# A graph layer with mixing attention and experts: scales of a group three stages late and fuller long rounds under the sort, contiguous one-hots, another end of layer two

## The reference

```python
xn = layernorm(x)
# graph part, two layers: mean over incoming edges, a linear layer, layer norm, SiLU
agg = segment_sum(h[src], dst) / maximum(degree, 1)
h = silu((layernorm(agg_plus_h @ W.T + b)) * g + beta)        # agg_plus_h = h + agg
# mix part (8 heads of 64): k, v = xn @ w_kv ; k and v are normalized over the 64 of each head
dots = sum_n k[n, h, :, None] * v[n, h, None, :]; out = (q @ dots / N) @ w_out.T + b_out
x = x + h + out
# experts: xf = layernorm(x); ONE routing decision from the mean of all rows of xf
logits = mean(xf) @ Wr + br                # softmax twice, the best 2 of 8 experts
x = x + layernorm(weighted sum of two experts' gelu MLPs(xf) + xf) * gamma + beta
```

## Time and profile before

| | us |
|---|---|
| median of 3 runs | 3044.67 (3039.23 to 3049.11) |
| the profiled execution | 3043.2 |
| its span in the trace | 3041.4 |
| DVE / PE / ACT / POOL busy | 1900.6 / 2552.5 / 1417.6 / 171.0 |

### The profile page before, as it was taken

How to read it: one execution, slowest core, us unless ns; L and a number is a source line. 1 busy time by engine, 2 the same in 40 slices (tenths; PEclk the granted TensorE clock), 3 DMA queues, 4 the chain that set the end, 5 groups by cost and what they waited for, 6 DMA issues and landing times. The chain is left out here.

```text
span 3041.4 us, 50876 instructions
## 1 busy us (share of the span) xinstructions
PE 2552.5 (84%) x14238; PEld 1577.4 (52%) x14238; DVE 1900.6 (62%) x4816; ACT 1417.6 (47%) x3756; POOL 171.0 (6%) x161
## 2 busy tenths in 40 slices
PE   1775664858688888889999999997999999968997
PEld 0343343424344454446578888884444444445665
DVE  8888978899899999999643222221333333355555
ACT  1875565257566666678622222222222222235665
POOL 0000000000000000000000000000111111114000
PEclk9888887889899999999999999998999999978999
DMA  5000000012144344344364444445444444401000
GB/s 179 18 18 9 15 15 15 35 61 98 73 156 149 114 154 144 120 148 141 139 226 144 154 147 145 149 143 194 136 136 140 135 136 138 140 1 38 28 21 30
DMA packets 167927, 318.02 MB, mean 105 GB/s; under 512 B 30227, under 2 KB 139540, under 8 KB 167764
## 3 DMA queue, kind: packets, MB, share of 16 engines
q1 hardware_dynamic: 115860, 230.55, 23.5%
q10 hardware_dynamic: 51776, 85.24, 7.7%
q0 software_dynamic: 128, 0.26, 0.0%
HBM read 203.09 MB, written 112.92 MB: 104 GB/s over the span
## 5 line engine op out<-in xcount | busy, mean ns | idle before, releaser
L1194 PE MATMUL banks<-outer,ring 128*128 128x512 f16 x2450 | 544.8, 381 | 16.0 <-DMA outer<-table,heavy 9.0
L825 ACT ACTIVATE ring<-banks 128x512 f16<-128x512 f32 (+1 forms) x637 | 367.0, 576 | 340.5 <-POOLq L676 337.3
L1191 PE MATMUL banks<-tabs,ring 128*128 128x257 f16 x2250 | 497.3, 273 | 2.5 <-DMA ring<-counts 2.5
L1192 PE MATMUL banks<-tabs,ring 128*128 128x256 f16 x2250 | 497.2, 272 | 0.0
L1194 PEld LDWEIGHTS banks<-outer,ring 128*128 128x128 f16 x2450 | 239.4, 98 | 302.3 <-issue 23.2
L826 ACT ACTIVATE banks<-banks 128x512 f32<-128x512 f32 (+1 forms) x637 | 368.6, 579 | 0.0
L1849 DVE TENSOR_SCALAR ring<-val,outer 128x512 f16<-128x512 f16 x1102 | 316.0, 345 | 39.6 <-PE banks L1157 38.7
L1157 PE MATMUL banks<-ring 128*128 128x512 f16 x920 | 270.4, 409 | 66.7 <-SPq L565 31.7
L969 PE MATMUL banks<-tabs,xT 128*128 128x512 f32 x400 | 201.9, 652 | 54.2 <-ACT xT L734 54.2
L1191 PEld LDWEIGHTS banks<-tabs,ring 128*128 128x128 f16 x2250 | 218.7, 97 | 32.7 <-DVE big L1887 2.2
L1192 PEld LDWEIGHTS banks<-tabs,ring 128*128 128x128 f16 x2250 | 219.5, 98 | 26.8
(11 more groups left out here) (368 smaller groups left out, 3939.4 us busy)
## 6 DMA issues: line engine op xcount, KB each, us to landing
counts<-ring ACTq DMA_DIRECT2D x84, 896.0 KB, 4.1
ring<-counts SPq DMA_DIRECT2D x94, 800.0 KB, 4.7
ring<-counts SPq DMA_DIRECT2D x94, 768.0 KB, 4.0
outer<-in_fw SPq DMA_DIRECT2D x8, 1024.0 KB, 8.1
outer<-in_x SPq DMA_DIRECT2D x5, 1280.0 KB, 13.5
x_transposed<-xT SPq DMA_DIRECT2D x50, 128.0 KB, 1.7
outer<-in_x SPq DMA_DIRECT2D x25, 256.0 KB, 2.9
xT<-x_transposed SPq DMA_DIRECT2D x25, 256.0 KB, 2.7
```

Of the source, the lines that this page charges most:

```text
L825: act.activation(held[:, b, 0:q, c, :], cell_bank.rearrange("p (q r) -> p q r", r=P), ACT.Copy, scale=0.25).then_inc(s_cell, 1)
L1191: mm(o[:, 0:D + 1], a, xtab[l][:, cb, D:2 * D + 1], start=cb == 0, stop=False)
L1192: m = mm(o[:, 0:D], a, xtab[l][:, cb, 0:D], start=False, stop=cb == NT - 1)
L1194: m = mm(o, a, xtab[l][:, cb, 0:2 * D], start=cb == 0, stop=cb == NT - 1)
```

## The change

Three parts, independent of each other.

**Mix under the sort.** `kv_norms` is cut in two: `kv_sums` (1503 and 1505 of before) stays at its tick; `kv_scales` (reciprocal and the multiplications of k) stands three ticks later in DVE's queue (in the rounds, right behind the sums as before). ACT's square root of a row window is moved behind the squares of the next window's first tile. The tiles of the rounds are dealt out anew: 4 to each of the odd rounds 1 to 11, and 2 to rounds 10, 12 and 13. PE has the dots of a window no longer ahead of the next even round's second turn half, but between the products of the tiles of the next odd round.

**One-hots.** `hot_c` is laid out with the column innermost, so that a step's weights are contiguous; `iota_c` is now 0..127 once, `col_v` holds every value twice (so that the innermost run of both inputs has two elements, the second input one value twice, and the value is read again for each of the 64 pairs).

**End of layer two.** The transposes of pair 23 stand inside the columns of the last tiles and its product behind those of tile 48; DVE's order for the last two pairs is written out; the affine of the last pair's normed rows is finished on DVE and not on POOL; xf's transposes use three banks in place of four; nine pairs (0 to 8) are transposed before the mean, 16 (9 to 24) behind the router's logits on PE, behind the third exponential on ACT and behind the routing weights on DVE.

```diff
+SCALE_LAG = 3
-WINDOWS = [2] * ROW_WINDOWS + [0, 3, 0, 3, 1, 3, 1, 3, 2, 3, 3, 3, 3, 2]
+WINDOWS = [2] * ROW_WINDOWS + [0, 4, 0, 4, 0, 4, 0, 4, 0, 4, 2, 4, 2, 2]
...
+XF_BANKS = (0, 1, 3)
+XF_LOWS = ((0, 2), (2, 3), (3, 5), (5, 7), (7, 9))
+XF_EARLY = XF_LOWS[-1][1]
...
                     kv_squares(t)
+                    if t == WSTART[w] and 0 < w < ROW_WINDOWS:
+                        kv_stds(w - 1)
...
             for w in range(ROW_WINDOWS):
                 window(w)
-                kv_stds(w)
+            kv_stds(ROW_WINDOWS - 1)
...
-                if w >= ROW_WINDOWS:
-                    dots_to(WSTART[w])
+                if WINDOWS[w] == 0:
+                    return
                 for t in range(WSTART[w], WSTART[w + 1]):
                     dots_to(t - 4)
                     kv_product(t)
...
+                if tick - SCALE_LAG in NORM_AT:
+                    kv_scales(NORM_AT[tick - SCALE_LAG])
                 if tick in NORM_AT:
-                    kv_norms(NORM_AT[tick])
+                    kv_sums(NORM_AT[tick])
...
-        hot_c = [v.bitcast(F16).rearrange("p (c k) -> p c k", k=8) for v in (ringf[:, 0:512], ringf[:, 512:1024], fvec[:, 0:512])]
+        hot_c = [v.bitcast(F16).rearrange("p (k c) -> p k c", k=8) for v in (ringf[:, 0:512], ringf[:, 512:1024], fvec[:, 0:512])]
...
-                dve.tensor_scalar(col_v[:, q % 2, 0:n], bank[5][:, 0:n], -64.0 * PB[q], None, op0=ALU.add)
+                dve.tensor_scalar(col_v[q % 2][:, 0:n, :], bank[5][:, 0:n].unsqueeze(2).to_broadcast([P, n, 2]), -64.0 * PB[q], None,
+                                  op0=ALU.add)
...
-                    dve.tensor_tensor(hot_c[t // 8 % 3], iota_c,
-                                      col_v[:, q % 2, u:u + 8].unsqueeze(1).to_broadcast([P, P, 8]), op=ALU.is_equal)
+                    dve.tensor_tensor(hot_c[t // 8 % 3].rearrange("p k (c u) -> p k c u", u=2),
+                                      iota_c.unsqueeze(1).to_broadcast([P, 8, P // 2, 2]),
+                                      col_v[q % 2][:, u:u + 8, :].unsqueeze(2).to_broadcast([P, 8, P // 2, 2]), op=ALU.is_equal)
...
-            dense(1, NP - 1, 0, 0, 0)
+            agg_free(1, NP - 1, 0)
+            slab_in(1, NP - 1, 0, 0)
+            columns(1, NP - 1, 0, 0, range(0, 12))
+            z_transposes(1, NP - 2, 1)
+            columns(1, NP - 1, 0, 0, range(12, HALF)).then_inc(s_half[1], 1)
+            product(1, NP - 2, 1)
             dense(1, NP - 1, 0, 0, 1)
...
-            for p in range(16, NP):
-                xf_transposes(p)
...
             mm(bank[6][:, 0:NE], ones[0:1, :], br_s[:, :], start=False, stop=True).then_inc(s_lg, 1)
+            for p in range(XF_EARLY, NP):
+                xf_transposes(p)
...
+            def last_pairs():
+                p, q = NP - 2, NP - 1
+                z_low(1, p, 1)
+                normal_h(1, p, 1)
+                z_tile(1, q, 0, 0)
+                dve.tensor_copy(stage[0][:, D:2 * D], tile(xn, NT - 1)).then_inc(s_z[1], 1)
+                outcome_sums(p, 1)
+                z_low(1, q, 0)
+                outcome_scaled(p, 1)
...
+                dve.tensor_tensor(two(tile(xn, q * 2, 2)), two(tile(xn, q * 2, 2)), both(gvec[1][1]), op=ALU.add).then_inc(s_gb[1], 1)
...
             link(dve.tensor_tensor(tw[1], e8[:, 0:1], tw[0], op=ALU.mult))
+            for p in range(XF_EARLY, NP):
+                xfT_low(p)
```

More of the change, by code:

```diff
@@ L709, in _ @@
             residual_beta(0)
-            with pool.Fori(2, NP) as p:
+            with pool.Fori(2, NP - 1) as p:
                 affine(1, p)
@@ L806, in _ @@
             act.wait_ge(s_nrm, NT)
-            act.activation(iota_c, iota16[:, 0:P].unsqueeze(2).to_broadcast([P, P, 8]), ACT.Copy, scale=0.5).then_inc(s_conv, 1)
+            act.activation(iota_c.rearrange("p c u -> p (c u)"), iota16[:, 0:P], ACT.Copy, scale=0.5).then_inc(s_conv, 1)
             for n, (a, scale) in enumerate(((0, 1.0), (2, 64.0), (1, 0.5))):
@@ L862, in xfT @@
                 act.wait_ge(s_ft, p + 1)
-                act.activation(xfp[:, p * 2:p * 2 + 2, 0:D], two(bank[p % 4]), ACT.Copy, scale=X_SCALE).then_inc(s_fc, 1)
+                act.activation(xfp[:, p * 2:p * 2 + 2, 0:D], two(bank[XF_BANKS[p % 3]]), ACT.Copy, scale=X_SCALE).then_inc(s_fc, 1)
             for n in range(2):
@@ L881, in second_layer @@
             def second_layer(p, b):
-                last = isinstance(p, int) and p == NP - 1
+                if isinstance(p, int) and p == NP - 1:
+                    zT(1, p, b)
+                    deviations(2, p - 1, 1 - b)
+                    for n in range(*XF_LOWS[0]):
+                        xfT(n)
+                    h_rows(1, p, b)
+                    deviations(1, p, b)
+                    for n in range(*XF_LOWS[1]):
+                        xfT(n)
+                    for n in range(*XF_LOWS[2]):
+                        xfT(n)
+                    silu(1, p)
+                    for n in range(*XF_LOWS[3]):
+                        xfT(n)
+                    deviations(2, p, b)
+                    return
                 zT(1, p, b)
-                if last:
-                    for n in range(4):
-                        xfT(n)
                 h_rows(1, p, b)
@@ L889, in second_layer @@
                 silu(1, p)
-                deviations(2, p, b)
+                if not isinstance(p, int) or p < NP - 2:
+                    deviations(2, p, b)
             pairs(act, second_layer)
-            for p in range(4, NP):
+            act.activation(small[:, 316:317], small[:, 317:318], ACT.Exp)
+            for p in range(*XF_LOWS[4]):
                 xfT(p)
-            act.activation(small[:, 316:317], small[:, 317:318], ACT.Exp)
             for n in range(3):
```

85 lines of the change are left out of this document (56 added, 29 removed).

## The result

| | before | changed |
|---|---|---|
| median | 3044.3 us (3039.23 to 3049.11, 4 runs) | 3011.68 us (3009.86 to 3013.41, 4 runs) |
| profiled execution, its span | 3043.2, 3041.4 us | 3013.41, 3011.7 us |

The ratio is 0.9893, 95% interval 0.9875 to 0.9911: the change makes the kernel 1.1% faster. I compare the two traces by five marks that both have.

A forecast was written before the change was run, and what follows sets the result against it. DVE's work bounds row stage, rounds and steps, a chain of small operations the end of layer two; 9 + 13 - 1 + 16 = 37 off 3043.2 gives 3006.2, as median 3008 us, range 2992 to 3025.

The forecast's parts named there:

- Row stage, 9 forecast: Row windows of the sort: moving scales and root lets 9 us of DVE's 12.9 us wait go, bounds 4 to 13.6.
- The wait for the squares: Row stage: DVE's wait in the sums for ACT's last squares falls from 12.9 to about 3 us.
- Rounds, 13 forecast (10 to 23): Rounds of the sort: redealt tiles and moved dots gain 13 us; 23 if the dots cost nothing, 10 if more.
- The pitch of 6.3: Odd rounds: dots between products add about 1 us to each tile's pitch, 6.3 in place of 5.15 us.
- the wait in the sums: Rounds: 23.3 us of wait go and 4 x 2.5 = 10 come back, in rounds 3, 5, 7 and 9.
- 3 x 2.24 = 6.7: Rounds 4, 6 and 8 without tiles: DVE waits for ACT's copy of their turn, 6.7 us lost.
- My term for the even turns: Rounds: turns of five even rounds no longer wait behind dots, some 0.7 us each of the 7.3, 3.7 gained.
- Steps, 1 slower forecast (3 slower to 4 faster): One-hot steps: `hot_c` keeps its duration, doubled `col_v` costs 2.3 us, contiguous weight loads gain 1.5: 1 us slower together.
- rival (c): Steps: `hot_c` loses its double rate or pays for the hops, total 3105 to 3155 us; chance 0.06.
- section 5.2's cost for single words: Steps, `hot_c`: about 0.65 cycle more per element without adjacent 4-byte words, estimated 347 ns a call, 95 us in all.
- End of layer two, 16 forecast: End of layer two: first expert product 16 us earlier, mean's row 20.5 earlier, late pairs 11.2 us; bounds 9 to 20.
- the 12 that I had named as a sign of being wrong: End of layer two: the prediction is wrong if the late pairs take over 12 us.

The follow-up runs named there:

- The fillers: Changed kernel plus PE transposes that compute nothing used, in empty even rounds: short ones 3005.03 us, long ones up to the next turn 3001.04 us.
- the dots put back: Changed kernel with the dots of an odd round's tiles back behind the next even round's turn: 2998.42 us, again 2998.54 us.
- dots back with fillers: Changed kernel with dots back behind the even rounds' turns and unused PE transposes behind them in rounds 4, 6 and 8: 2996.56 us.

## Why the prediction was right, and where it was not

The total was right (3008 forecast, 3011.68 measured, inside 2992 to 3025, 32.6 faster against 36), but one of its four terms was four times too large. By the two traces the gain is 29.7 against 37: the rounds gave 10 less, the steps 3 more. That the median lies within 4 us of the forecast is in part luck: the steps erred the other way, and the medians differ by 3 us more than the two profiled executions.

- **Row stage, 9 forecast, 9.3 measured** (8.9 when undone). The wait for the squares fell to 2.7 us, as I had put it; that the root would be waited for longer (5.1 in place of 2.5) was not in my sum. Both waits together fell by 7.6, and by 8.2 between the marks (the first window's wait, 1.85 and 2.42, lies ahead of them); where the other 1.1 comes from, the groups don't show. The mechanism was right, the exact hit is luck.
- **Rounds, 13 forecast (10 to 23), 3 measured.** The pitch of 6.3 was right (6.32), the wait in the sums came to 12.8 for 10. The step that failed is "rounds 4, 6 and 8 have no tile, so that ACT's copy of their turn is waited for, 3 x 2.24 = 6.7": 4.5 us became 20.3, not 11.2. I had priced an odd turn by rows in which PE came from a tile's work or had idled little (1.97 us). The change leaves PE idle for 12 to 15 us ahead of the turns of rounds 5, 7 and 9, and for 2.7 and 5.0 ahead of those of rounds 1 and 3, where dots stood before. These five turns take 3.4 to 3.7, and DVE waits 3.6 to 3.8 for each in place of 2.24: 7.4 us. The other 1.6 are short waits in rounds 11 and 13, which my sum did not have. The first product behind the turn takes 4.8 to 4.9 for 3.70 in rounds 3 and 5, and their sums wait 3.6 where those of rounds 7 and 9 wait 2.4. The fillers and the dots put back show it. My term for the even turns was wrong in its reason too: a turn has 16 transposes, 8 for each half, so the order rows ahead of the prediction show whole turns of rounds 2 and 3, not two halves of one, and no even turn stood behind dots. Its wait before is the turn itself, at the low level (3.40 to 3.68 us in rounds 2 to 12); it fell from 7.3 to 1.4 because the scales of a fourth tile and the longer wait in the sums cover it.
- **Steps, 1 slower forecast (3 slower to 4 faster), 2.1 faster measured**, 3.5 alone. The double rate holds at 683 ns, so rival (c) is out. Two other traces with the changed kernel's rounds show about 2 us as well, the nine others with these one-hots 4.5 to 7. Of the Trainium skill's page "Vector Engine (DVE) Microarchitecture Reference", section 5.1 (two elements in a run suffice) agrees with these 683 ns, and section 5.2's cost for single words, as I had applied it, does not show in them. Mis-sized was the worth of the shorter weight loads: DVE waits 3 to 7.5 us less for the step products.
- **End of layer two, 16 forecast, 15.7 measured.** The late pairs took 12.7 for 11.2, over the 12 that I had named as a sign of being wrong (their last low half starts at 12.0), the hand-over to the mean's row was 2.9 for 2.4, the router 10.7 for 11.5, the end of the columns, counted from the last one-hot, moved by 5.8 for 3.8, and the chain from there to xf took 19.0 for 19.7. The first expert product came 14.2 us earlier, counted so; my 16 had, besides, a slip in its last addition (2728.5 + 1.1 + 2.48 is 2732.1, not 2731.7). The experts took 1.6 less, which the kernel with the one-hots alone shows as well (1.3), so that it is most likely not this part's. The part is worth some 14 us, as it is alone, and that the marks give 15.7 for 16 is luck.

The sum of the parts taken alone or undone, 8.9 + 1 + 3.5 + 14.2 = 27.6, against 28.6 to 32.6 for the whole on the chips tried: within the noise nothing speaks against their being independent.

## What to carry to other kernels

Moving TensorE's work out of a stretch leaves it at the low level for the next thing that others wait for (here a turn of 3.68 us in place of 1.97): price that thing by a row in which PE comes from as long an idle time, not by the nearest row of its kind. When work is dealt anew, look at what now stands between two links of the densest loop: here moving dots back to where PE idles was worth 13 us, more than the dealing itself, some 8 of them for the loop and the rest for the shorter idle times and the steps. And work that needs no result of a wait (the 16 late pairs, 12.7 us) is cheaper where a load is in flight anyway: here by 6.3 us to the first expert product and 7.5 by the medians.

## What the runs showed of the hardware

- In six traces (before, changed, dots back, short and long fillers, dots back with fillers) the 17 turns of 16 transposes that came behind 0.3 to 1.8 us of idle PE took 1.95 to 1.97 us, and the 37 behind 3.9 to 14.8 us of idle took 3.1 to 3.7. Between 2.3 and 3.8 us of idle both durations occur (1.97 behind 2.94, 3.41 behind 2.65), so these runs give no fixed limit.
- The turn of round 5 in the changed kernel had a granted clock of 0.50 (3.68 us), the one before the change 1.00 (1.97 us).
- DVE's double rate for two-byte values held with three patterns whose innermost run is two elements as the kernel writes them, one of them two equal neighbours that are read again 64 times: 683 ns for 1,024 values.
- A contiguous weight load takes 98 ns where one with a stride of eight two-byte values took 146; in the kernel with the one-hots alone it is 98 as well.
